# Position bias of a windowed attention: from four full matmuls on TensorE to a per-partition bias on ScalarE and 24-column corrections

## The reference

```python
K, H, D = 7, 16, 8                       # window, heads, width of a head
ni   = clip(pos - K // 2, 0, L - K)      # first key of a token's window, L = 92
idx  = ni[:, None] + arange(K)           # its 7 keys
bias = rpb[:, idx - pos[:, None] + (K - 1)]
attn = einsum('bhld,bhlkd->bhlk', q, k[:, :, idx]) + bias
attn = softmax(attn, axis=-1)
```

## Time and profile before

| | |
|---|---|
| median of 3 runs | 832.96 us (832.21 to 834.46) |
| profiled execution, span from the first to the last instruction | 837.2 us |
| PE busy | 635.0 us (76% of the span) |
| VectorE busy | 631.0 us (75%) |
| ScalarE busy | 524.3 us (63%) |
| GpSimd busy | 281.6 us (34%) |
| mean granted TensorE clock | 0.875 of full speed |

### The profile page before, as it was taken

The page is one execution under the profiler, slowest core; times in us unless marked ns, Lnnn a source line. Parts: engine busy times, 40 slices in busy tenths (PEclk is TensorE's granted clock), DMA queues, the critical chain, the costliest instruction groups (busy, mean ns, idle before and its releaser), DMA issues.

```text
span 837.2 us, 11023 instructions
## 1 busy us (share of the span) xinstructions
PE 635.0 (76%) x3178; PEld 489.5 (58%) x3179; DVE 631.0 (75%) x1271; ACT 524.3 (63%) x837; POOL 281.6 (34%) x313
## 2 busy tenths in 40 slices
PE   6998652653717355389767899988899999999998
PEld 4554652653717355275545589844667667667665
DVE  1786597999999999997874312167798898997853
ACT  1588999999899898982232134352575565575452
POOL 0465000000010000000377244416356666664552
PEclk9998876967769586789666799999999999999999
DMA  5380044344445554441411366320000000000000
GB/s 182 121 303 20 1 85 72 72 86 86 80 76 103 100 104 79 72 72 60 163 30 33 92 179 179 100 69 0 1 1 10 1 10 8 3 11 6 5 10 19
DMA packets 26384, 56.52 MB, mean 68 GB/s; under 512 B 4203, under 2 KB 15572, under 8 KB 25860
## 3 DMA queue, kind: packets, MB, share of 16 engines
q0 software_dynamic: 5728, 24.56, 15.6%
q1 hardware_dynamic: 19848, 30.80, 12.2%
q10 hardware_dynamic: 764, 0.62, 0.2%
HBM read 29.91 MB, written 10.17 MB: 48 GB/s over the span
## 4 chain that ended last, share of the span: by engine, by line
PE 39%; DVE 28%; issue 15%; ACT 11%; DMA 3%; SPq 2%; POOL 2%; another core or an unknown queue 1%; DVEq 0%; ACTq 0%; POOLq 0%
PE psum L2035 5%; DVE s_R L1265 3%; DVE s_R L1252 3%; PE psum L1749 3%; DVE s_R L1276 2%; PE psum L1951 2%; PE psum L2022 2%; PE psum L1959 2%; PE psum L1821 2%; PE psum L1822 2%; PE psum L1823 2%; PE psum L2091 2%; PE psum L2023 2%; PE psum L2024 2%; PE psum L2068 2%
## 5 line engine op out<-in xcount | busy, mean ns | idle before, releaser
L1821 PE MATMUL psum<-s_xn_lo,s_split_hi 128*128 128x368 f32 x256 | 95.0, 371 | 137.6 <-ACT s_R L911 134.8
L1821 PEld LDWEIGHTS psum<-s_xn_lo,s_split_hi 128*128 128x128 f32 x256 | 54.7, 214 | 142.3 <-ACT s_R L911 137.5
L671 POOL DMA_DIRECT2D s_xnfm<-s_R x14 | 17.1, 1219 | 257.3 <-DVE s_R L1276 257.3
L1271 DVE TENSOR_TENSOR_SCAN s_R<-s_R 128x2944 f32<-128x2944 f32 x16 | 100.7, 6292 | 0.8
L1047 ACT ACTIVATE s_R<-psum,s_cols 128x368 f32<-128x368 f32 x96 | 49.5, 566 | 70.2 <-PE psum L2024 70.1
L1822 PE MATMUL psum<-s_xn_hi,s_split_lo 128*128 128x368 f32 x256 | 92.1, 360 | 0.0
L1823 PE MATMUL psum<-s_xn_hi,s_split_hi 128*128 128x368 f32 x256 | 91.6, 358 | 0.0
L2035 PE MATMUL psum<-s_R 128*128 128x368 f32 x256 | 90.1, 478 | 0.0
L767 POOL TENSOR_TENSOR s_R<-s_R 128x368 f32<-128x368 f32 x48 | 46.7, 974 | 61.8 <-DVE s_R L1676 60.0
L730 POOL TENSOR_TENSOR s_R<-s_R 128x368 f32<-128x368 f32 x47 | 54.2, 1154 | 38.1 <-DVE s_R L1546 20.0
L918 ACT ACTIVATE s_R<-psum,s_cols 128x736 f32<-128x736 f32 x64 | 56.1, 876 | 14.0 <-PE psum L1823 10.1
(11 more groups left out here) (256 smaller groups left out, 1654.7 us busy)
## 6 DMA issues: line engine op xcount, KB each, us to landing
s_xnfm<-s_R POOLq DMA_DIRECT2D x14, 1472.0 KB, 10.5
s_R<-in_w SPq DMA_DIRECT2D x28, 256.0 KB
s_R<-in_xg SPq DMA_DIRECT2D x7, 744.0 KB, 4.1
x_sorted<-in_x_init SPq DMA_DIRECT2D x1, 5082.0 KB
s_wBC<-in_wBC SPq DMA_DIRECT2D x8, 256.0 KB, 2.8
s_R<-in_v SPq DMA_DIRECT2D x2, 1024.0 KB
s_R<-x_sorted SPq DMA_DIRECT2D x28, 66.0 KB
s_R<-in_w SPq DMA_DIRECT2D x1, 1536.0 KB, 6.8
```

What stands on the lines that cost most here:

```text
L1271: dve.tensor_tensor_scan(bufB[:, u], ra[:, u], bufB[:, u], 0.0, ALU.mult, ALU.add).then_inc(ra_free, 1)
L1821: pe.matmul(bank(c), w_hi[:, s, u, k, :], xn_lo[:, a:b], start=True, stop=False)
```

## The change

ScalarE's copy of the scores becomes an `Identity` activation with a per-partition bias: the seven inner biases of the 16 heads, one number for each of the 112 rows, in a new last column of `cols`. `posc` now has -1 in the row of the inner kind wherever the token is not an inner one, and nothing for inner tokens, so that its matmul gives the difference from the inner bias. That matmul is made only at the 24 columns (4 sequences x 2 ends x 3 tokens) where it isn't zero. The four short matmuls come behind the head sums of the first four offsets, each behind the one of its own quarter, since these now start the sums in PSUM.

```diff
-             ("C_b", NS), ("b1", 2 * NE), ("delta_b", 1), ("gate_b", 1)]
+             ("C_b", NS), ("b1", 2 * NE), ("delta_b", 1), ("gate_b", 1), ("rpb_mid", 1)]
...
-                act.activation(S_fm, bank(3, OH), ACT.Copy).then_inc(S_ready, 1)
+                act.activation(S_fm, bank(3, OH), ACT.Identity, bias=col("rpb_mid")[0:OH], scale=1.0).then_inc(S_ready, 1)
...
+            def edges(x):
+
+                return bass.AP(x.tensor, x.offset, [list(x.ap[0]), [L, CB], [L - K // 2, 2], [1, K // 2]])
+
             def scores(c):
                 pe.wait_ge(qkv_ready, c * 3 + 3)
-                for q in range(4):
+                for o in range(K):
+                    q, only = o % 4, o < 4 and o + 4 >= K
                     m = min(32, OH - 32 * q)
-                    pe.matmul(quarter(q), rpb_w[:, 32 * q:32 * q + m], posc, start=True, stop=False)
-                for o in range(K):
-                    m = min(32, OH - 32 * (o % 4))
                     pe.wait_ge(prod_r, c * K + o + 1)
-                    ins = pe.matmul(quarter(o % 4), sel[:, o, 0:m], prod[:, o], start=False, stop=(o + 4 >= K))
+                    ins = pe.matmul(quarter(q), sel[:, o, 0:m], prod[:, o], start=(o < 4), stop=(o >= 4))
+                    if o < 4:
+                        ins = pe.matmul(edges(quarter(q)), rpb_w[:, 32 * q:32 * q + m], edges(posc),
+                                        start=False, stop=only)
                     if o + 4 >= K:
                         ins.then_inc(S_mm, 1)
...
+    t["cols"][0:K * HEADS, -1] = rpb_w[K // 2]
...
-    t["posc"] = c_(np.tile((first[None] == np.arange(K)[:, None]).astype(f), (1, CB)))
+    away = (first[None] == np.arange(K)[:, None]).astype(f)
+    away[K // 2] -= 1
+    t["posc"] = c_(np.tile(away, (1, CB)))
```

More of the change, by code:

```diff
@@ L2228 @@
         np.broadcast_to(a["L0_attn_delta_b"].reshape(1, 1), (D, 1)),
-        np.broadcast_to(a["L0_attn_gate_b"].reshape(1, 1), (D, 1))], axis=1))
+        np.broadcast_to(a["L0_attn_gate_b"].reshape(1, 1), (D, 1)), np.zeros((D, 1), f)], axis=1))
     t["rows"] = c_(np.broadcast_to(np.stack([a["L0_tok_gamma"], a["L0_tok_beta"], a["L1_attn_proj_b"],
```

## The result

The changed kernel takes 851.86 us (median of 4 runs, 851.43 to 852.53) where the kernel before took 833.07 (832.21 to 834.46): a ratio of 1.0211, 95% interval 1.0192 to 1.0229. It is 18.8 us slower. The forecast was 851.2, in a range of 843 to 860.

A forecast was written before the change was run, and what follows sets the result against it. The prediction took PE's score matmuls, on the chain in every steady turn, to set the pace. Six steady turns at 2.35 + 0.07 us, plus 1.3 and 2.4, made 18.2; added to 832.96 this gave 851.2, range 843 to 860.

The forecast's parts named there:

- The borders: Among PE's score matmuls, eight changes between 7 x 32 and 128 x 32 stationaries each hold the next load; 2.35 us more per steady turn.
- The first rival: No drain between the two 32-column shapes in PE's score matmuls: stretch 1.50 instead of 2.11 us, time 829.9; chance 6%.
- Its size: PE's scores in a steady turn: four times 0.74 plus 0.19, then 0.74, make 4.46 us against 2.11.
- The copy: ScalarE's copy of the scores grows from 478 to 568 ns; some 0.07 us of it shows per steady turn.
- Turn 0: First turn of the attention stage: sums follow late products, the copy comes 1.2 us later, 1.3 with its slower form.
- Turn 1: Second attention turn: 0.7 us later at full clock, with the copy; 2.4 with a low-clock stretch as long as before.
- the term of 1.7 us: In turn 1, a low-clock stretch as long as before, 3.41 us, costs half of that, 1.7 us.
- The clock in the steady turns: Turns 2 to 7: PE is busy nearly throughout, so the granted clock was expected to stay at 1.00.
- The second rival: Thinner PE work makes the clock fall to 0.50 in each steady turn: 10 us more, 861; chance 7%.
- The sum: Over the attention turns: six steady turns make 14.5 us; with 1.3 and 2.4 for the first two, 18.2 us.
- against the profiled span of 837.2 that is 855.4: Whole kernel: 18.2 us added to the profiled span gives 855.4; the median of the runs was 4.2 us lower.

The follow-up runs named there:

- one shape: Changed kernel in its own order, short matmuls' stationary padded with zeros from 7 to 128 rows; 831.82 us, ratio to before 0.9969; repeated 831.48 us, 0.9960.
- Copy alone: Kernel before with only ScalarE's copy of the scores made an Identity activation with a bias column of zeros; 833.80 us beside 834.40, ratio 0.9992.

## Why the prediction was right

**The borders: right.** The step on which all hung, that each change between 7 and 128 rows holds the next load until the earlier passes are done, was read from one border of the kernel before. The five waits of 0.60 us (one is 0.61) in the timeline after show it, and "one shape" takes four of them away with nothing changed but rows of zeros. The first rival (no drain between the shapes) is out by the same pair of runs. The Trainium skill has it so in TensorEngine Tiling (Array Packing), "Key Properties": a change of tiling mode drains. The trace agrees, with 0.60 us of waiting for a load at each border behind a sum of 368 columns; that 7 rows after 128 are such a change is what "one shape" shows, the page does not name the case. What the Trainium skill's other page (TensorE: Matmul & The Clock Gate, "Part 3: Packing small matmuls") says of matmuls at different positions holds here within a shape: eight loads within 0.17 us in "one shape".

**Its size: nearly.** A sum with its border took 0.72 to 0.74 us for 0.74, an edge 0.15 to 0.17 for 0.19, the last round 0.74 for 0.74. Stretch 4.33 for 4.46, 2.22 more than before for 2.35.

**The copy: right in length, wrong in effect.** 568 ns as forecast, but none of the 0.07 us a turn came through. I took ScalarE for the one that releases the exponential because L1022 ends at 650.04 and the exponential starts at 650.10. VectorE's L1602 ends beside it, at 650.06:

```profile
649.11 0.95 DVE L1602 TENSOR_TENSOR s_R<-psum,s_R 92x448 f32<-92x448 f32 x1
```

In the changed kernel, turn 3, ScalarE:

```profile
650.81 0.57 ACT L1068 ACTIVATE s_R<-psum,s_cols 112x368 f32<-112x368 f32 x1 [5.14 <-PE psum L2093]
651.39 1.28 ACT L806 ACT_TABLE_LOAD   x1
...
652.80 1.64 ACT L1022 ACTIVATE s_xs<-s_H,s_R,s_rs 92x128 f32<-92x128 f32 x4
654.39 0.58 ACT L1075 ACTIVATE s_R<-s_R 92x448 f32<-92x448 f32 x1
```

and VectorE:

```profile
653.40 0.96 DVE L1602 TENSOR_TENSOR s_R<-psum,s_R 92x448 f32<-92x448 f32 x1
```

L1602 ends at 654.36, the exponential starts at 654.39. L1022 by its record ends only at 654.44, when the exponential has already started, so its end is not what the exponential waited for. From copy to exponential it is 3.58 us, before it was 3.59, though the copy is 0.09 longer: VectorE's line was the later one, and ScalarE had at least that much to spare. "Copy alone" shows the same.

**Turn 0: right.** The copy comes 7.61 us after the first q matmul (549.38 to 556.99), before 6.43 (552.86 to 559.29): 1.18 for the 1.2 forecast.

**Turn 1: near, in part by chance.** From turn 0's copy to turn 1's it is 26.53 us; it was 24.44 in the first profile of before and 23.82 in the second: 2.1 and 2.7 us for the 2.4 forecast. The two profiles of before are not alike there. The windows of turn 1 in the second one have no fall of the clock:

```profile
570.47:573.88 3.41, 2.13 (x16) 0.59 (x16) 3.34 (x16) 0.00 (x0) 1.99 (x1) 1.00 0.00 0
573.88:577.29 3.41, 2.84 (x16) 1.16 (x15) 3.20 (x13) 1.30 (x2) 2.85 (x5) 1.00 0.00 0
```

Behind 2.13 us of PE work in 3.41 the clock fell in one execution and held in the other. So the thin stretch, which the prediction put ahead of the fall, does not by itself explain it; what does stays open, and that the term of 1.7 us was due in the profiled execution is luck. Only the 2.1 compares a fall with a fall. The windows of the changed kernel:

```profile
574.13:577.54 3.41, 1.31 (x10) 0.94 (x8) 3.34 (x13) 0.99 (x2) 1.86 (x2) 1.00 0.00 0
577.54:580.95 3.41, 3.38 (x9) 0.90 (x10) 3.38 (x9) 0.00 (x0) 3.25 (x3) 0.50 0.00 0
580.95:584.36 3.41, 2.68 (x16) 0.72 (x15) 0.91 (x7) 0.82 (x2) 2.23 (x6) 1.00 0.00 0
642.00:676.00 34.00, 32.12 (x157) 21.91 (x157) 28.24 (x82) 19.04 (x39) 20.87 (x22) 1.00 0.02 7
```

and its first weight loads of turn 1:

```profile
577.54 0.18 PEld L2093 LDWEIGHTS psum<-s_R 128*32 128x32 f32 x2 [2.32 <-issue]
578.90 0.18 PEld L2095 LDWEIGHTS psum<-s_R 7*32 7x32 f32 x2 [1.18 <-issue]
```

PE was busy for 1.31 us of the 3.41 before its first sum. The granted clock was 0.50 (1.2 GHz) from that sum on, at 577.54, and a sum with its border took 1.36 us there; in rows 12 the clock fell at 580.46, 0.8 us into the sums. It was back at 1.00 from 580.95, for sums 3 to 6. The low stretch was as long as in rows 12, 3.41 us. From first load to copy it is 5.98 us (577.54 to 583.52), in turn 3 it is 4.52 (646.29 to 650.81): the fall cost 1.5 us for the 1.7 forecast.

**The clock in the steady turns: it held.** The last of the windows above, turn 3, has 1.00, and so has the trace from 598.10 us to 850.40:

```profile
598.10:850.40 252.30, 234.59 (x1131) 162.32 (x1129) 193.29 (x547) 131.18 (x261) 137.20 (x151) 1.00 0.02 7
```

The second rival did not come.

**The sum, and what it was added to.** The terms came to 18.2 us. Measured over the last stage they are 301.1 - 284.3 = 16.8, or 17.2 against the second profile: 1.0 to 1.4 us less: 0.8 is the smaller stretch (6 x 0.13) and 0.4 the copy (6 x 0.07); turn 1 is uncertain by 0.6. The first profile and the changed kernel's both have the fall in turn 1, the second has none there, so 16.8 is the better comparison. The runs differ by 18.8, which is 1.6 to 2.0 us more than the last stage shows. Where that rest comes from is not shown, but further runs of the kernel before give a hint. Its 833.07 us are 4 runs; beside the experiments it took 834.40 (25 runs) and 834.93 (23 runs), and against these the changed kernel is 17.5 and 16.9 us slower, as its last stage has it. It did not run beside them, and the start of the last stage moves by more than 2 us between executions of one kernel, so no run here tells whether the change shifts that start. So the 0.7 us between 851.2 and 851.86 is luck: the terms came out 1.0 to 1.4 us too high, and the rest of 1.6 to 2.0, which the forecast knew nothing of, offset that.

One step failed: "against the profiled span of 837.2 that is 855.4". The span after is 850.5. I had put the 4.2 us between the first span and the median down to profiling. In fact the time of an execution is some 1.8 us over its own span (852.27 and 850.5; 831.46 and 829.6), and the first profile had caught an execution whose last stage began 3 to 7 us later than in the other profiles shown here. The sum had to be made against the length of the last stage.

## What to carry to other kernels

Matmuls that run beside each other in different quarters of the array did so here only while their stationaries had the same number of rows (16 columns beside 32 did no harm); each visit from 128 rows to 7 cost some 0.17 us and, worse, began a new round of some 0.75 us, however few matmuls the round had. When a small matmul must go between packed ones, pad its stationary with zero rows to their shape, or gather all such matmuls in one place at a border that is there anyway; fewer columns bought nothing while each short matmul stood between two sums. And compare profiles over the stage that the change touches: here whole spans of one unchanged kernel lay 7.6 us apart, while the last stage repeated within 0.5.

## What the runs showed of the hardware that was not expected

Dead rows cost less than a change of shape: an edge whose stationary has 128 rows, 121 of them zeros, adds less here than one of 7 rows. Four of them with the sums of the same shape need 1.45 us, the seven sums alone with their border 1.37; four of 7 rows at the end need 1.55. And a border is priced by what it interrupts: behind sums the wait for a load is 0.60 us, while behind the edges, whose passes are short, the profile lists none, and edge and border together take 0.17 us.
